# Loading and preparing layer 1's block weights during layer 0's mixture of experts

## What is computed

```python
xn = _layernorm(x)
s = _L0_attn_ref(xn, ...)        # gated delta rule, 16 heads of 64
g = _silu(_L0_ffn_ref(xn, ...))  # 8 experts, the 2 best of each token
x = x + s * g
xn = _layernorm(x)
s = _L1_attn_ref(xn, ...)        # attention beside a state-space scan, then an MLP
g = _silu(_L1_ffn_ref(xn, ...))  # 8 experts, balanced assignment
x = x + s * g
```

## Time and profile before

| | us |
|---|---|
| median of 3 runs | 4683.19 |
| lowest and highest of them | 4669.66, 4691.1 |
| profiled execution | 4703.35 |
| its span, first to last instruction | 4701.6 |
| PE busy | 3809.9 (81%) |
| DVE busy | 2623.9 (56%) |
| ACT busy | 1833.6 (39%) |
| POOL busy | 1183.0 (25%) |

### The profile page before, as it was taken

How to read it: one execution, slowest core, us unless ns; L and a number is a source line. 1 busy time by engine, 2 the same in 40 slices (tenths; PEclk the granted TensorE clock), 3 DMA queues, 4 the chain that set the end, 5 groups by cost and what they waited for, 6 DMA issues and landing times. The chain is left out here.

```text
span 4701.6 us, 133275 instructions
## 1 busy us (share of the span) xinstructions
PE 3809.9 (81%) x60410; PEld 2933.3 (62%) x60410; DVE 2623.9 (56%) x4402; ACT 1833.6 (39%) x2937; POOL 1183.0 (25%) x1148
## 2 busy tenths in 40 slices
PE   5888888888888888888889999924777888777855
PEld 4777777777777787777878888822333334333424
DVE  5345354453544535445325555544877888888743
ACT  2333333234232333323326666522444454444422
POOL 2221322312213123131234555361000000000063
PEclk7999999899998999989999999956888898988878
DMA  5341010000000000000025444311212211221214
GB/s 192 122 138 57 14 30 13 23 20 12 22 17 17 11 12 19 7 17 11 14 92 171 150 162 151 125 48 41 55 45 55 64 54 51 55 59 50 59 37 130
DMA packets 206516, 284.72 MB, mean 61 GB/s; under 512 B 86712, under 2 KB 148416, under 8 KB 199808
## 3 DMA queue, kind: packets, MB, share of 16 engines
q1 hardware_dynamic: 136160, 111.25, 8.8%
q0 software_dynamic: 24016, 107.80, 7.0%
q10 hardware_dynamic: 45776, 57.15, 3.6%
HBM read 215.59 MB, written 72.61 MB: 61 GB/s over the span
## 5 line engine op out<-in xcount | busy, mean ns | idle before, releaser
L869 DVE TENSOR_TENSOR sd_z<-psum,sd_z 128x512 f32<-128x512 f32 x320 | 219.0, 688 | 414.4 <-PE psum L737 414.4
L2765 PE MATMUL psum<-ss_h,ident 128*128 128x512 f32 x512 | 300.9, 718 | 21.8 <-DVE ss_h L2880 21.4
L2874 DVE TENSOR_TENSOR_SCAN ss_h<-ss_da,ss_h 128x1024 f32<-128x1024 f32 x128 | 294.8, 2303 | 3.5 <-ACT ss_da L2814 3.0
L916 POOL TENSOR_TENSOR sd_z<-id,s_up 128x512 f32<-128x512 f32 x64 | 81.3, 1271 | 848.3 <-DVE s_up L875 847.7
L1783 PE MATMUL psum<-e_h,e_mid_w 128*128 128x256 f32 x1248 | 283.9, 381 | 2.0 <-DMA e_mid_w<-table_mid,r_table_i 2.0
L2522 POOL TENSOR_TENSOR at_qs<-at_q,slot_of 128x512 f32<-128x512 f32 x32 | 44.5, 1399 | 952.8 <-ACT at_q L2392 708.0
L1783 PEld LDWEIGHTS psum<-e_h,e_mid_w 128*128 128x128 f32 x1248 | 238.7, 191 | 34.6 <-issue 2.4
L737 PE MATMUL psum<-sd_z,s_do 64*64 64x64 f32 x6144 | 225.2, 229 | 27.6 <-ACT s_do L818 26.8
L737 PE MATMUL psum<-s_low,s_up 64*64 64x64 f32 x6144 | 224.2, 225 | 27.8 <-DVE sd_z L869 22.2
L737 PEld LDWEIGHTS psum<-sd_z,s_do 64*64 64x64 f32 x6144 | 207.2, 143 | 62.6 <-issue 33.5
L2435 ACT ACTIVATE x_tok<-psum 128x512 f32<-128x512 f32 x320 | 165.2, 603 | 195.7 <-PE psum L2360 195.5
(11 more groups left out here) (472 smaller groups left out, 9915.5 us busy)
## 6 DMA issues: line engine op xcount, KB each, us to landing
ss_rows<-bc_scratch SPq DMA_DIRECT2D x128, 512.0 KB, 4.8
answered<-ce_zeros ACTq DMA_DIRECT2D x19, 1024.0 KB, 5.2
routed<-ce_zeros ACTq DMA_DIRECT2D x16, 1024.0 KB, 9.3
st_eg<-gate_scratch SPq DMA_DIRECT2D x128, 128.0 KB, 5.3
table_mid<-in_t_mid ACTq DMA_DIRECT2D x4, 1536.0 KB, 7.7
m_w<-in_m_w ACTq DMA_DIRECT2D x16, 256.0 KB, 7.4
table_down<-in_t_down ACTq DMA_DIRECT2D x1, 2560.0 KB, 12.2
g_x<-in_x SPq DMA_DIRECT2D x8, 256.0 KB, 6.0
```

The lines of the kernel that those rows point to most:

```text
L869: dve.tensor_tensor(d.z[:, :, :], bank[:, :].rearrange("p (a t) -> p a t", a=NP), d.z[:, :, :], ALU.add).then_inc(T.dve.give(r, name), 1)
L916: pool.tensor_tensor(D[m % 3].z[:, :, :], w["id64"][:, :].unsqueeze(1).to_broadcast([P, NP, C64]), T.up[:, :, :], ALU.subtract).then_inc(T ...
L2765: t = pe.matmul((b5, b6)[m][:, :], w["ident"][:, :], Z.h_of(b, n)[:, m, :], start=False, stop=(n == DS - 1), skip_group_check=True)
L2874: dve.tensor_tensor_scan(flat, flat2(Z.da[n % 2][:, :, :]), flat, 0.0, ALU.mult, ALU.add).then_inc(Z.dve.give(b, f"s{n}"), 1)
```

## The change

The 26 loads and the preparation of layer 1's block move into `layer0_mixture`. Their tiles are now allocated by `layer1_memory`, ahead of the mixture and on the outer stack, so they are memory of their own during the mixture, some 14,000 bytes of each partition (3,500 float32 numbers; the narrow tiles counted too). They keep their place behind the tiles of `Layer1`, and in the same order; the block's own tiles come behind them as before, those of the mixture and of layer 1's experts lie that much further on.

SP issues the loads once line 0 has finished its second tile (`X[0].dve.at(1, "out")`). ACT and DVE find their part between the last tile and the sums. The block's engines no longer wait for the loads themselves, only for `prepared`.

```diff
--- before.py
+++ after.py
@@ -2092,6 +2092,8 @@
     tiles_act(C, X)
     tiles_dve(C, X)
     tiles_pool(C, R, X, tables, routed, answered)
+    nc.sync.wait_ge(*X[0].dve.at(1, "out"))
+    prepared = layer1_weights(C, ins)
     for x in X:
         nc.gpsimd.wait_ge(*x.put.now())
     nc.vector.wait_ge(*xn_in.now())
@@ -2105,6 +2107,7 @@
         nc.sync.wait_ge(*Y.dve.at(b, "out"))
         nc.sync.dma_start(x1_dram[b].rearrange("(c p) h -> p c h", p=P), C.x_tok[:, b * CH:(b + 1) * CH, :]).then_inc(*L.spilled.up())
     fence(C, Y.dve.at(NB + 1, "sc"), Y.act.at(NB, "nc"))
+    return prepared
 
 
 
@@ -2127,19 +2130,32 @@
         self.spilled, self.x_back = C.loads("x_spilled"), C.loads("x_back")
 
 
+WEIGHTS1 = [*[(name, [P, 1]) for name in ("pre_w", "pre_b", "mid_w", "mid_b", "q_b", "k_b")],
+            ("q_w", [P, H]), ("k_w", [P, H]), ("v_w", [P, H]), ("o_w", [P, H]), ("ssm_out_w", [P, DB, H]),
+            ("in_proj_w", [P, 2 * DI]), ("conv1", [P, DB, 4]), ("conv1_b", [P, DB]), ("x_proj_w", [P, DB, DTR + 2 * DS]),
+            ("dt_w", [DTR, DI]), ("dt_b", [P, DB]), ("a_log1", [P, DB, DS]), ("d_param", [P, DB]), ("ffn_w1", [P, FF]), ("ffn_b1", [P, FB]),
+            ("ffn_w2", [P, FB, H])]
+ROWS1 = ["v_b", "o_b", "mix", "ffn_b2"]
+
+
+def layer1_memory(C):
+
+    w = C.w
+    for name, shape in WEIGHTS1:
+        w[name] = C.sb(name, shape)
+    for name in ROWS1:
+        w[name] = C.sb(name, [P, H])
+    w["neg_a1"], w["slot_of"], w["skip"] = C.sb("neg_a1", [P, DB, DS]), C.sb("slot_of", [P, 4]), C.sb("skip", [P, DB, P])
+
+
 def layer1_weights(C, ins):
+
     nc, w = C.nc, C.w
     loads = C.loads("weights1")
-    load_weights(C, ins, loads, [
-        *[(name, [P, 1]) for name in ("pre_w", "pre_b", "mid_w", "mid_b", "q_b", "k_b")],
-        ("q_w", [P, H]), ("k_w", [P, H]), ("v_w", [P, H]), ("o_w", [P, H]), ("ssm_out_w", [P, DB, H]),
-        ("in_proj_w", [P, 2 * DI]), ("conv1", [P, DB, 4]), ("conv1_b", [P, DB]), ("x_proj_w", [P, DB, DTR + 2 * DS]),
-        ("dt_w", [DTR, DI]), ("dt_b", [P, DB]), ("a_log1", [P, DB, DS]), ("d_param", [P, DB]), ("ffn_w1", [P, FF]), ("ffn_b1", [P, FB]),
-        ("ffn_w2", [P, FB, H])])
-    for name in ("v_b", "o_b", "mix", "ffn_b2"):
-        w[name] = C.sb(name, [P, H])
+    for name, _ in WEIGHTS1:
+        nc.sync.dma_start(w[name][tuple(slice(None) for _ in w[name].shape)], ins[name]).then_inc(*loads.up())
+    for name in ROWS1:
         nc.sync.dma_start(w[name][:, :], ins[name].partition_broadcast(P)).then_inc(*loads.up())
-    w["neg_a1"] = C.sb("neg_a1", [P, DB, DS])
     act, dve = nc.scalar, nc.vector
     ready = C.steps("prep1", ["a", "m", "neg", "add", "inv", "ow", "ob", "rest", "slot", "skip0", "skip1", "ssm"])
     act.wait_ge(*loads.now())
@@ -2158,14 +2174,12 @@
     dve.wait_ge(*ready.at(0, "ob"))
     dve.tensor_scalar(w["mix"][:, :], w["mix"][:, :], -1.0, 1.0, ALU.mult, ALU.add).then_inc(ready.give(0, "rest"), 1)
     dve.wait_ge(*ready.at(0, "rest"))
-    w["slot_of"] = C.sb("slot_of", [P, 4])
     dve.tensor_reduce(w["slot_of"][:, :], w["head_of"][:, :].rearrange("p (r s) -> p s r", s=4), AX.X, ALU.add).then_inc(ready.give(0, "slot"), 1)
-    w["skip"] = C.sb("skip", [P, DB, P])
     for m in range(DB):
         dve.tensor_scalar(w["skip"][:, m, :], w["ident"][:, :], w["d_param"][:, m:m + 1], None, ALU.mult).then_inc(ready.give(0, f"skip{m}"), 1)
     dve.tensor_tensor(w["ssm_out_w"][:, :, :], w["ssm_out_w"][:, :, :], w["mix"][:, :].unsqueeze(1).to_broadcast([P, DB, H]),
                       ALU.mult).then_inc(ready.give(0, "ssm"), 1)
-    return loads.now(), ready.at(0, "ssm")
+    return ready.at(0, "ssm")
 
 
 def rsqrt(C, rstd, mv, steps, r, added, name):
@@ -3235,12 +3249,10 @@
     dve.tensor_copy(R.slot_i[:, :], G.slot_f[:, :]).then_inc(last.give(0, "done"), 1)
 
 
-def layer1_block(C, R, ins, bc_dram, routed, order):
+def layer1_block(C, R, prepared, bc_dram, routed, order):
     nc = C.nc
-    loaded, prepared = layer1_weights(C, ins)
     A, Z, T, G = Attention(C), StateSpace(C), Tail(C), Selection(C)
     for engine in (nc.tensor, nc.scalar, nc.vector, nc.gpsimd):
-        engine.wait_ge(*loaded)
         engine.wait_ge(*prepared)
 
     nc.scalar.wait_ge(*R.spilled.now())
@@ -3471,15 +3483,16 @@
         C.stack = whole
         C.x_tok = C.sb("x_tok", [P, NT, H])
         R = Layer1(C)
+        layer1_memory(C)
         x_in = [C.loads(f"x_in{b}") for b in range(NB)]
         for b in range(NB):
             nc.scalar.dma_start(C.x_tok[:, b * CH:(b + 1) * CH, :], ins["x"][b].rearrange("(c p) h -> p c h", p=P)).then_inc(*x_in[b].up())
         with ExitStack() as C.stack:
-            layer0_mixture(C, routing, R, ins, x_in, (ins["t_up"], t_mid, t_down), routed0, answered0, xn_dram, x1_dram)
+            prepared = layer0_mixture(C, routing, R, ins, x_in, (ins["t_up"], t_mid, t_down), routed0, answered0, xn_dram, x1_dram)
         with ExitStack() as layer1:
             C.stack = layer1
             with ExitStack() as C.stack:
-                layer1_block(C, R, ins, bc_dram, routed, order)
+                layer1_block(C, R, prepared, bc_dram, routed, order)
             with ExitStack() as C.stack:
                 layer1_experts(C, R, ins, outs, routed, answered, order, x1_dram)
```

## The result

The changed kernel takes 4670.42 us (median of 20 runs, 4660.79 to 4681.86) against 4686.99 us (20 runs, 4669.66 to 4700.83): ratio 0.9962 with a 95% interval of 0.9952 to 0.9972, so 17.8 us less (13.1 to 22.5); the two medians lie 16.6 us apart. The forecast was 20.3 us less. The profiled execution after took 4660.79 us, the fastest of its 20 runs, with a span of 4659.0 us, which is 42.6 us less than the span before; what that adds to some 20 us will turn out to be no effect of the change.

A forecast was written before the change was run, and what follows sets the result against it. All engines waiting at the fence for layer 1's weight loads and preparation was taken as the bound: 20.7 us removed less 0.4 for POOL's scatters gives 20.3, from median 4683.19 to 4662.9 us; range 4646 to 4680.

The forecast's parts named there:

- The stall removed: Between layer 0's last copy of the scores and layer 1's block: the block starts 20.7 us earlier.
- The covers: Idle or waiting times in the mixture and block expected to hide the moved loads, preparation and added table load at 0 us.
- The collision of gathers: In the mixture: the moved loads delaying the tile-weight gathers, tightest down_w with 3.8 us of slack; taken as 0.
- the collision case: Rival: three lines each lose 11.1 us to late gathers, 33 us in all, giving 4695.6 us; chance 0.03.
- ACT's and DVE's covers: After the last tile: idle times of 24.56 and 16.00 us hide 1.9 us of ACT and 3.1 of DVE; cost 0.
- The added table load: Before the attention's first exponential: 1.28 us of reloading hidden in ACT's 4.85 us idleness; 0, or 1.3 us if uncovered.
- POOL's pauses: At the block's start, around POOL's reduction: 5.75 and 7.46 us, shifting unchanged; 1.7 us kept for the range.
- The price of POOL's scatters: Ahead of the sums: two scatters stretched by DVE's preparation beside them; between 0 and 1.8 us, 0.4 taken.
- the row of 1.43 us: In the sums: a POOL gather taking 1.43 us beside two tensor_tensors, 0.95 beside a quiet DVE; basis for 0.4 us.
- Its rule on tensor_scalar: Ahead of the sums: the preparation's five tensor_scalars would block POOL about 1 us instead of 0.4, time 0.6 us later.
- The clock: Rival: without PE's stillness the block starts nearer the 2.4 GHz level, up to 12 us more gained, 4651; chance 0.10.
- a returning wait: Rival: thinner cover ahead of the sums or longer POOL pauses take back 10 to 20 us, 4673 to 4683; chance 0.12.

The follow-up runs named there:

- late_prep: Changed kernel with the loads still early but ACT's and DVE's preparation back behind the fence; ratio to the kernel before 0.9959 (0.9946 to 0.9972).
- late_loads: Changed kernel with the 26 loads issued only after the last tile, preparation still ahead of the sums; ratio to the kernel before 0.9965 (0.9950 to 0.9979).
- loads_x8: Changed kernel with the 26 loads issued eight times over in the mixture, 12 MB; first to last tile 598.2 us, no ratio given.
- hold: Changed kernel plus 26 idle tiny loads all engines wait for between fence and block; engines stand still 17.1 us more, no ratio given.

## Why the prediction was right

**The stall removed.** Forecast 20.7 us; copy to at_x fell from 21.0 and 20.9 to 0.2 us. The release after the fence takes 0.04 us where 0.08 was allowed. late_prep and late_loads show its parts: 17 us for the loads and 4 for the preparation. The working had 15.7 (3218.60 less 3202.99 is 15.6), 2.0 and 3.1; its split is right except that 1.3 us of ACT's part, the table load, would have vanished with the loads alone.

**The covers.** The collision of gathers was priced at 0: loads_x8 shows that even eight times as much costs 0.5 to 0.8 us. (The price of the collision case, 4695.6, adds up to 4695.9 with its own 33 us.) ACT's and DVE's covers held, and late_loads shows that DVE's is a real one: it has some 13 us and not more. The added table load is covered. POOL's pauses stayed, so nothing had run ahead during the wait.

**The price of POOL's scatters** was the term that was mis-sized: 0.4 us forecast, 0.07 measured (1.03 against 0.96 for the second, the first unchanged). It is real: the second takes 1.02 to 1.03 us in the nine runs with the preparation beside it and 0.95 to 0.96 in the four without. The working took the row of 1.43 us as the price of lying beside two tensor_tensors. At 3102.92 only one was running, `x_tok` of 128x512 since 3102.84, and what it costs is how long it still runs. Rows of two pairs from the sums after the change and one from those of late_loads show it:

```profile
3088.18 0.95 POOL L1981 DMA_INDIRECT e_h<-answered,r_slot  x1 [0.30 <-issue]
3088.32 0.69 DVE L2069 TENSOR_TENSOR x_tok<-x_tok,e_hid 128x512 f32<-128x512 f32 x1
...
3098.08 0.69 DVE L2069 TENSOR_TENSOR x_tok<-x_tok,e_hid 128x512 f32<-128x512 f32 x1
3098.13 1.46 POOL L1981 DMA_INDIRECT e_h<-answered,r_slot  x1 [0.30 <-issue]
```

```profile
3106.30 0.69 DVE L2067 TENSOR_TENSOR e_hid<-e_hid,s 128x512 f32<-128x512 f32 x1 [2.03 <-ACT e_hid L2005]
3106.64 1.17 POOL L1981 DMA_INDIRECT e_h<-answered,r_slot  x1 [0.30 <-issue]
```

The gather of 3088.18 starts 0.14 us before DVE's tensor_tensor and takes 0.95 us beside all its 0.69 us. The gather of 3098.13 starts 0.05 us after one, with 0.64 us of it left, and takes 1.46. That of 3106.64 has 0.35 us left and takes 1.17. The second scatter starts at 3068.78 with 0.19 us left of the tensor_tensor of 3068.69, and takes 1.03. These three end 0.82 or 0.83 us after the tensor_tensor does. In the 13 profiles, 639 indirect DMAs of POOL start 0.04 us or more after a tensor_tensor with both inputs in SBUF and with at least 0.18 us of it left, and every one of them ends 0.81 to 0.87 us after it. Of the 91 gathers beside `x_tok`, the three that started 0.01 us after it took 0.94 or 0.95, and the 18 that started ahead of it 0.94 to 0.99, with one of 1.17, the one above, which the tensor_tensor before had held. The longest scatter of the run before, 1.85 us, had 1.0 us left of one of 128x1024. So the scatters were never threatened by the 0.48 us of the row: the preparation's own tensor_tensors last 0.28 to 0.42 us.

The Trainium skill has both halves: page "SBUF — State Buffer", section "Who interferes with whom", says that issue order and not the op's shape decides who blocks, which these rows bear out; the same section's expectation that tensor_tensor leaves descriptor writing alone, which it calls inferred, is not borne out. Its rule on tensor_scalar, by which the working would have added 0.6 us, was not put to the test here: the three that lie beside the second scatter (3069.01, 3069.37) all started after it.

**The clock** was given 0.10 for up to 12 us more, and the interval of 13.1 to 22.5 us leaves no room for 32. Its mechanism does not show where it was to act: the granted clock is 0.50 in the sums and 0.67 in the block's first 20 us in all five profiles of the table and in hold, with or without the pause. A small part of it may be there. The first scan comes 2.1 to 2.5 us later in hold than without the pause, but its block as a whole is 3.6 to 3.9 us shorter. With one profile each, and blocks that vary by 12 us, it is not shown that any of it reaches the end.

**The rivals of a returning wait and of colliding loads** fall with the table of stages: no row but one differs between the kernels by more than between two profiles of one kernel.

**The number.** 4662.9 us was forecast, 4670.42 measured, inside the range. Of the 7.5 us, 3.8 come from the starting point (the median of three runs, 4683.19, against 4686.99 of twenty), the other 3.7 from medians that lie 16.6 us apart instead of 20.3. The ratio says 17.8 us with an interval that holds 20.3, and the profiles' stretch from the last result to at_x says 20.3. "Within 0.5%" is what came: the gain is 0.38%.

## What to carry to other kernels

Read a fixed wait behind a fence as its whole length, and price it by the stretch between two instructions that both kernels have, not by the spans of two profiles: here the spans differed by 42.6 us, the stretch by 20.8 us, and the runs by 17.8. Loads moved into a long matmul stage cost nothing that shows, and eight times as many less than 1 us at a DMA share of 0.80, so what had to be chosen with care here is only that they end before the preparation's cover begins. And after removing one wait at a fence, look at what bounds the first product behind it: here a reduction across partitions on POOL, whose replacement by two small PE products brought the first scan 6 to 7 us forward. On that chip the median fell by another 10.5 us, with intervals that still overlap.

## What the runs showed of the hardware

- The reduction across partitions is surrounded by two pauses of POOL, 5.6 to 6.7 us ahead of it and 6.6 to 7.8 us behind, with no instruction in them, and both vanish with it. The Trainium skill, page "GPSIMD Engine Reference", tells of about 6 us for the first call to freshly loaded code, with no visible instruction; the first pause agrees in size, the second is somewhat longer. What fills them was not shown.
- An indirect DMA instruction of POOL that starts 0.04 us or more inside a DVE tensor_tensor with both inputs in SBUF ends 0.81 to 0.87 us after it (639 of 639 with at least 0.18 us of it left): 1.46 us with 0.64 left, 1.03 with 0.19 left. One that starts ahead of the tensor_tensor, even by 0.03 us, takes its usual 0.95.
- An ACT table load runs ahead of a wait that sits on the activation behind it: at a fence whose last wait was for DVE it ran at 3192.98, the activation at 3195.11 us (late_prep).
- With the code unchanged, the stage ahead of the mixture ends between 2419.9 and 2437.9 us in the five profiles of the table. PE's granted clock over the first 2400 us is 0.92 in the two latest of the five and 0.93 or 0.94 in the others, so the clock goes with it there; it is not all of it, since loads_x8 has 0.92 too and ends at 2423.7. The 594 us of tiles, in which PE stands only for 7.8 us, near their end, take 594.3 to 594.4 us in every profile of two chips and of the first two profiles, and 597.5 to 597.7 us on another (598.2 with the eightfold loads).
